# A graph-network kernel of four layers on one core: one store per batch instead of four, and a rearranged first norm and second batch norm

## Time and profile before

| what | value |
|---|---|
| median of 3 runs | 464.56 us (463.43 to 468.84) |
| time of the profiled execution | 463.99 us |
| its span, first to last instruction | 462.2 us |
| busy: PE, DVE, ACT, POOL | 442.4, 340.3, 241.0, 38.4 us |
| mean granted clock of PE | 0.984 |
| moved by DMA | 99.23 MB |

### The profile page before, as it was taken

One profiled execution on the slowest core, in us unless ns is written; L12 is line 12 of the kernel. 1 busy time (PEld: TensorE's weight loads), 2 busy tenths in 40 slices (PEclk: granted clock), 3 DMA queues, 4 the chain that ended last, 5 costly groups with the idle time before them and its releaser, 6 DMA issues.

```text
span 462.2 us, 6176 instructions
## 1 busy us (share of the span) xinstructions
PE 442.4 (96%) x2202; PEld 273.4 (59%) x2202; DVE 340.3 (74%) x725; ACT 241.0 (52%) x421; POOL 38.4 (8%) x59
## 2 busy tenths in 40 slices
PE   5999999899899999999999999999599999999996
PEld 3434434344343334878776866676267688888885
DVE  3897876899999969879779657675758785866212
ACT  3998784586798634663335436445542533511210
POOL 3330000012311200010010000100000000000000
PEclk8899999999999999999999999999889999999999
DMA  7997535123999999856099766772990740000002
GB/s 261 417 365 170 198 116 211 61 92 142 357 397 403 379 386 384 328 164 246 0 358 423 292 238 255 279 251 71 401 340 26 296 150 34 1 0 2 0 3 91
DMA packets 18906, 99.23 MB, mean 215 GB/s; under 512 B 3903, under 2 KB 4287, under 8 KB 8383
## 3 DMA queue, kind: packets, MB, share of 16 engines
q1 hardware_dynamic: 14151, 72.86, 42.2%
q0 software_dynamic: 4000, 25.18, 14.8%
q10 hardware_dynamic: 720, 0.73, 0.5%
HBM read 93.50 MB, written 5.25 MB: 214 GB/s over the span
## 4 chain that ended last, share of the span: by engine, by line
PE 82%; DMA 10%; DVE 6%; issue 1%; ACT 1%; DVEq 0%; SPq 0%; ACTq 0%
PE bank L1270 18%; PE sbank L1592 9%; DMA bring<-in_basis 9%; PE sbank L1256 8%; PE bank L1343 7%; PE sbank L1326 6%; PE bank L1605 6%; PE bank L1498 5%; PE bank L1577 5%; PE bank L1256 3%; PE bank L1310 3%; PE sbank L1236 3%; PE sbank L1310 3%; PE sbank L1381 2%; PE bank L1404 2%; PE sbank L1458 2%
## 5 line engine op out<-in xcount | busy, mean ns | idle before, releaser
L1256 PE MATMUL sbank<-bring,attw 120*32 120x512 f32 x320 | 40.3, 612 | 4.9 <-DMA bring<-in_basis 4.9
L762 DVE TENSOR_SCALAR cnt<-iota_row,edge_f 128x512 bf16<-128x512 f16 x132 | 40.8, 345 | 4.4 <-PE sbank L1326 4.4
L509 ACT ACTIVATE adjT<-distance,edge_w,edge_f 128x128 bf16<-128x128 bf16 x61 | 29.2, 480 | 2.0 <-PE sbank L1326 2.0
L1326 PE MATMUL sbank<-cnt,adjT 128*128 128x512 bf16 x132 | 30.0, 380 | 0.0
L419 ACT ACTIVATE stat<-stat,eps 128x1 f32<-128x1 f32 x32 | 9.4, 295 | 39.0 <-DVE stat L772 39.0
L1343 PE MATMUL bank<-hT,wring 128*128 128x512 f32 x64 | 28.9, 594 | 0.0
L1185 DVE SCALAR_TENSOR_TENSOR y_lo<-sbank,gate,y_hi 128x512 fp32r<-128x512 f32 x16 | 11.8, 749 | 22.6 <-ACT y_hi L690 22.6
L448 ACT ACTIVATE s<-bank,colsb 128x512 f32<-128x512 f32 x24 | 16.4, 687 | 21.8 <-PE bank L1270 21.8
L1256 PE MATMUL bank<-bring,attw 120*32 120x512 f32 x192 | 23.7, 600 | 2.6 <-DMA bring<-in_basis 2.5
L759 DVE TENSOR_SCALAR adjT<-iota_row,edge_f,edge_w 128x128 bf16<-128x128 f16 x71 | 22.1, 311 | 5.4 <-PE sbank L1326 5.4
L480 ACT ACTIVATE distance<-iota_row,edge_f 128x128 bf16<-128x128 f16 x61 | 24.3, 400 | 1.7
(11 more groups left out here) (227 smaller groups left out, 1062.8 us busy)
## 6 DMA issues: line engine op xcount, KB each, us to landing
bring<-in_basis SPq DMA_DIRECT2D x63, 1024.0 KB, 8.2
wring<-in_weights POOLq DMA_DIRECT2D x8, 1024.0 KB, 10.0
landing<-in_weights POOLq DMA_DIRECT2D x4, 1024.0 KB, 7.2
w_scratch<-stage SPq DMA_DIRECT2D x64, 64.0 KB, 8.0
hT<-in_weights POOLq DMA_DIRECT2D x4, 1024.0 KB, 10.4
qkw<-w_scratch POOLq DMA_DIRECT2D x2, 2048.0 KB, 8.1
rring<-in_rows POOLq DMA_DIRECT2D x12, 256.0 KB, 8.6
hT<-w_scratch POOLq DMA_DIRECT2D x4, 256.0 KB, 6.9
```

The costliest lines, as they stand in the source:

```text
L509: act.activation(hot_d[:, n % HOT, :], distance[:, i % 2, :], ACT.Relu, scale=minus_w[:, n:n + 1], bias=weight_f[:, n:n + 1]).then_inc(sem ...
L762: dve.tensor_scalar(hot_s[:, n % HOT, :], iota[:, :], src_f[:, n:n + 1], None, ALU.is_equal).then_inc(sem("hot_ready"), 1)
L1256: mm = pe.matmul(unit_bank(b)[32 * j:32 * j + 32, :], attw[0:KB, u // UNITS, g, :], bring[0:KB, u % BATCH, j, :], start=(g == 0), stop=(g ...
L1326: pe.matmul(bank[7][:, :], hot_d[:, n % HOT, :], hot_s[:, n % HOT, :], start=(n == 0), stop=(n == ECH - 1)).then_inc(sem("hot_used"), 1)
```

## The change

- **Stores.** SP stores a batch with one DMA instead of four. Its DRAM side has three dimensions, 4 x 32 x 512 elements, its SBUF side is 128 partitions of 512. The store of batch n // 4 - 2 is issued ahead of the load of unit n, no longer behind it. The semaphore that tells of a stored batch counts 16 instead of 64.
- **First norm.** POOL writes `eps` first. ACT takes a square root of it as soon as its DMAs are issued, into a tile that nobody reads. Square roots and the scaled ReLUs go in pairs of tiles. ACT copies turned tiles 2 and 3, DVE copies tiles 0 and 1. PE turns into banks 0 to 3, with 23 zero matmuls ahead and 0, 4, 1, 2 behind the four turns (12 and 2, 2, 2, 2 before). The first q tile comes ahead of all counts.
- **Second batch norm.** Two units instead of four stand ahead of the turns. Behind them come four units, two zero matmuls, one unit and three zero matmuls (three units before).

```diff
@@ stored()
-            return sum(b % SLOTS == slot for b in range(groups)) * COLT * 16
+            return sum(b % SLOTS == slot for b in range(groups)) * 16
@@ SP, for n in range(2 * UNITS + 2 * BATCH)
+                    if n % BATCH == BATCH - 1 and n >= 3 * BATCH - 1:
+
+                        b = n // BATCH - 2
+                        sp.wait_ge(sem("stage_ready"), b + 1)
+                        layer, g = divmod(b, BATCHES)
+                        if b == 2 * BATCHES - 1:
+                            sp.wait_ge(sem("gate_rows"), 16 * 2 * RELS)
+                        sp.dma_start(scratch[layer].rearrange("(j u) q o -> j u q o", j=COLT)[
+                            :, g * BATCH:(g + 1) * BATCH, :, :].rearrange("j g q o -> j (g q) o"),
+                            stage[:, b % SLOTS, :]).then_inc(
+                                sem(f"w_stored{b % SLOTS}"), 16)
                     if n < 2 * UNITS:
...
-                        for j in range(COLT):
-                            at = j * UNITS + g * BATCH
-                            sp.dma_start(scratch[layer, at:at + BATCH, :, :].rearrange("g q o -> (g q) o"),
-                                         stage[32 * j:32 * j + 32, b % SLOTS, :]).then_inc(
-                                             sem(f"w_stored{b % SLOTS}"), 16)
@@ POOL: memset(eps) is first, ahead of memset(zeros)
@@ ACT
+                act.activation(root_of_eps[:, :], eps[:, :], ACT.Sqrt)
+
+                def relu0(c):
                     act.wait_ge(sem("nbias0"), c + 1)
...
+                root(0, 0)
+                root(0, 1)
+                relu0(0)
+                relu0(1)
+                root(0, 2)
+                root(0, 3)
+                relu0(2)
+                relu0(3)
+                for c in (2, 3):
+                    turn("hT0", hT, c, 0, C)
@@ DVE
                 for c in range(C):
                     dve.wait_ge(sem(f"x{c}_loaded"), 16)
-                    n = step(dve.bn_stats(st(0, c, 0, 6), xr[:, c, :]))
-                    if c:
-                        nbias(0, c - 1)
-                    after(n)
-                    norm_aggr(0, c)
-                nbias(0, C - 1)
+                    norm_stats(0, xr[:, c, :], c)
+                    if c == 1:
+                        nbias(0, 0)
+                        nbias(0, 1)
+                nbias(0, 2)
+                nbias(0, 3)
+                for c in (0, 1):
+                    dve.wait_ge(sem("hT0_psum"), c + 1)
+                    dve.tensor_copy(hT[:, :, blk(P, c)],
+                                    bank[c][:, :].rearrange("p (f n) -> p f n", f=C)).then_inc(sem("hT0"), 1)
@@ PE, start
-                keep_clock(12)
+                keep_clock(23)
                 pe.wait_ge(sem("ident"), 2)
-                for c in range(C):
-                    turn(hr, c, "h0", "hT0")
-                    keep_clock(2)
+                for c, idle in enumerate((0, 4, 1, 2)):
+                    turn(hr, c, "h0", "hT0", base=0, banks=C)
+                    keep_clock(idle)
+                pe.wait_ge(sem("hT0"), C)
+                qkv_tile(0)
                 for n in range(ECH):
                     count(n)
-                    if n == first:
-                        pe.wait_ge(sem("hT0"), C)
                     t, at = divmod(n - first, every)
+                    if t == 0:
+                        continue
@@ PE, second batch norm
                 parts_stage("c2_1", x_parts, "c1_1", "c2_1_psum")
-                units(4)
+                units(2)
...
-                units(3)
+                units(4)
+                keep_clock(2, bank[4])
+                units(1)
+                keep_clock(3, bank[4])
```

More of the change, by code:

```diff
@@ L207, in build @@
         eps = sb("eps", [P, 1])
+        root_of_eps = sb("root_of_eps", [P, 1])
         distance = sb("distance", [P, 2, P], BF16)
@@ L326, in _ @@
             def _(pool):
+                pool.memset(eps[:, :], LN_EPS).then_inc(sem("eps"), 1)
                 pool.memset(zeros[:, :], 0.0).then_inc(sem("zeros"), 1)
@@ L330, in _ @@
                           allow_small_or_imprecise_dtypes=True).then_inc(sem("iota"), 1)
-                pool.memset(eps[:, :], LN_EPS).then_inc(sem("eps"), 1)
                 pool.memset(ones[:, :], 1.0).then_inc(sem("constants"), 1)
@@ L489, in _ @@
                 act.wait_ge(sem("eps"), 1)
-                for c in range(C):
-                    root(0, c)
+                act.activation(root_of_eps[:, :], eps[:, :], ACT.Sqrt)
+                def relu0(c):
                     act.wait_ge(sem("nbias0"), c + 1)
@@ L494, in _ @@
                                    bias=st(0, c, 10)).then_inc(sem("h0"), 1)
-                    if c:
-                        turn("hT0", hT, c - 1)
-                turn("hT0", hT, C - 1)
+                root(0, 0)
[8 more added lines that the diff above has]
+                    turn("hT0", hT, c, 0, C)
                 act.wait_ge(sem("edge_step"), 8)
@@ L1346, in _, with keep_clock @@
                 first, every = FIRST_TILE, TILE_EVERY
-                def keep_clock(n):
+                def keep_clock(n, to=bank[7]):
                     for _ in range(n):
-                        pe.matmul(bank[7][:, :], zeros[:, 0:P], zeros[:, :], start=True, stop=True)
+                        pe.matmul(to[:, :], zeros[:, 0:P], zeros[:, :], start=True, stop=True)
                 pe.wait_ge(sem("zeros"), 1)
-                keep_clock(12)
+                keep_clock(23)
                 pe.wait_ge(sem("ident"), 2)
-                for c in range(C):
-                    turn(hr, c, "h0", "hT0")
-                    keep_clock(2)
+                for c, idle in enumerate((0, 4, 1, 2)):
[3 more added lines that the diff above has]
+                qkv_tile(0)
                 for n in range(ECH):
                     count(n)
-                    if n == first:
-                        pe.wait_ge(sem("hT0"), C)
                     t, at = divmod(n - first, every)
+                    if t == 0:
+                        continue
                     if at == 0 and t < 2 * C:
```

## The result

The changed kernel takes **475.22 us** (median of 4 runs, 474.80 to 475.93) against 464.78 for the kernel before (4 runs, 463.43 to 468.84). The ratio of the means is 1.021, with a 95% interval of 1.015 to 1.028: slower, by about 2%. The forecast was 468.4, its range ended at 473.0. The profiled execution after took 475.93 with a span of 474.1; before it was 462.2.

What follows compares the result with a forecast made beforehand. PE holds 82% of the chain of waits, with PE, DVE and DMA nearly full in the attention. 463.99 - 3.0 (start) + 4.0 (attention) + 1.5 (unit 43) + 1.9 (second batch norm) = 468.4 us, range 456.5 to 473.0.

Steps and rivals of the forecast that it cites:

- The mechanism of the store: Stores: one DMA with four shared outermost pieces goes over four engines, 64 KB each, +1.9 us for each batch.
- Rival A: Whole kernel: the store is spread over all 16 engines and everything works as written, -6.5, 457.5 us; chance 0.25.
- If all 6.0 are slack the cost is 1.5, if none is 7.5 ... +4.0: Attention, to unit 29: dearer stores delay loads; unit 29 started 6.0 us after the loads' floor; +4.0 us taken.
- 2.5 to 5 later, +1.5, bounds 0 and +2.5: Unit 43: its load, now behind the store, lands 2.5 to 5 us later, at 249.5 to 252, wanted at 249.4.
- The start: First norm: earlier table load and ReLUs bring the first q tile and counts forward, -3.0 us, bounds -1.6 and -3.3.
- the 23 zero matmuls fill PE until about 7.7: Start: the zero matmuls ahead of the turns last until about 7.7 us, when the first ReLU ends.
- The 6 us for DVE's 16 one-hots: Start: 16 counts need 6 us of DVE, until 19.3; PE wants the last at 19.2, so DVE just keeps up.
- The second batch norm: Second batch norm: unit 59's load waits behind a store, three zero matmuls follow, clock stays low; +1.9, bounds -3.0 and +3.5.
- An earlier start of PE is therefore kept: From the start to 80 us: PE has no wait on the chain, so its gain stays as far as DVE starts earlier.
- Rival B: Attention: four engines set its whole pace, slower by over 2%, 476.9 us, or 475.5 with the full start; chance 0.10.
- part 3: The prediction's part on the second batch norm: +1.9 us forecast, +3.5 in rival B.
- Rival C: Start: it does not pay, -1.0 instead of -3.0, while the store costs as forecast; 470.4 us; chance 0.10.

## Why the prediction was wrong

**The mechanism of the store held.** The store goes over four engines, its issue takes 0.5 us, and unit 59's load decides at the second batch norm. Rival A is out in both of its halves: the store is not spread, and where it is spread (462.9 us, contiguous rows) it is not faster than four stores in the same place (463.9) by more than their intervals, where A had 457.5. The Trainium skill, page "DMA: Bandwidth & Descriptors", section "Rules for kernel authors", advises to merge small transfers. Here merging 64 KB stores into one of 256 KB gave nothing that could be measured on 16 engines, and cost 11 us on four (in the same place, ahead of the load).

**The steps that failed are two sizes and a term that was left out, 7.6 us in all.**

1. *The attention: "If all 6.0 are slack the cost is 1.5, if none is 7.5 ... +4.0".* Measured +6.1 up to unit 29, and +6.6 with the one store behind the load. The bounds held, but I took a value near the middle, with no row for it: of the 7.5 us that four stores add to four engines I counted 3.5 as slack. The five kernels with a store on four engines lost 5.3 to 6.8 us from unit 0 to unit 29, so only 0.7 to 2.2 were slack. With two engines the same sum gives 17.5 us, and the trace 16.1, so 1.4 were slack. With eight it gives 2.5, and the trace nothing. That is an estimate by my own price for a byte, and it fits: the cost is near nothing while the rings still have room, and nearly the full bytes once they have not.

2. *What a wait leaves behind was left out, although the rows had it.* I priced the lower clock at the second batch norm (0.81, 2.00 for four matmuls), and not at the two places where I was making new waits. Behind unit 29 unit and projection took 0.87 + 2.17 = 3.0 us more (that this is the clock is argued, not tried), of which 0.6 came back later; behind unit 43 the clock took 1.6, and filling that wait with zeros gave this back in the trace. Together 4.1 of the 7.6, for a term that stood in the sum at nothing.

3. *Unit 43, "2.5 to 5 later, +1.5, bounds 0 and +2.5".* The load took 5.0 us more (19.06 against 14.1), the upper end of the span, and I had taken the lower half. The shift from the wait alone came to 2.8 us, over the bound, and the clock's 1.6 came on top.

Two sizes were off by less. The start gave 2.3 and not 3.0: "the 23 zero matmuls fill PE until about 7.7" held in the run with four stores (6.42 us, to 7.8) and failed in the changed kernel's profile (8.00 us, to 9.35). From 4 to 7 us TensorE ran 9 of the zero matmuls there, and 16 in the other run. The granted clock is told as 1.00 for that stretch in both, so a lower clock that lasted longer is likely and not shown. Over the 13 profiles with the changed start unit 0 begins between 22.93 and 23.93 us, which is a gain of 2.0 to 3.0: 3.0 was the upper end. The 6 us for DVE's 16 one-hots do not follow from the rates given (16 x 0.345 and DVE's half of the other kind give about 8); in the run with four stores behind, the chain goes through them from 12.49 to 19.41, so DVE just kept up, as forecast. The second batch norm cost 1.3 and not 1.9.

"An earlier start of PE is therefore kept" failed too, though the sum hides it. With stores on four engines, unit 36 starts at 235.1 to 235.6 us with the changed start and without it.

**Rival B** is the one that came true in its result: 475.5 with the full start, against 475.22. It got 0.10. Its own marks were passed only in part: unit 29 at 171.6, not beyond 172, and its +7.5 there was really 6.1 up to unit 29 and 2.5 behind it. It also had +3.5 in part 3, where 1.3 came, and +2.5 at unit 43, where 4.5 came. The number came out right partly by luck, and the chance was still too low: B needs only that little slack is left, and a DMA share of 0.99 is a row that says so. Rival C is out as the cause: the first q tile began at 12.85, short of its 14.

## What to carry to other kernels

Before merging DMAs, count the outermost pieces of both sides of the merged one: if fewer than 16 come out, some engines get several times the bytes, and a load that is spread over all 16 lands with the slowest. Where the rings are nearly full, price those bytes in full as soon as they exceed what little room there is: 16 KB more on an engine for each store cost 0.7 us here, 32 KB on top 11, and 64 KB on top 18. Check too that a gain ahead of such a stretch gets through it. And where a change adds waits on TensorE, price the matmuls behind them at the lower clock as one bound; if a wait can't be avoided, zero matmuls in it can give the clock back (1.6 us in the trace here).

## What the runs showed that I had not expected

- The count of packets on the page tells how many engines a DMA used: 16 x 12 = 192 fewer for 16 stores on 4 engines, to the packet; and a store on fewer than 16 engines has no landing time on the page. Its semaphore has one update for each engine and one more.
- An outer count written over rows that follow on each other changes nothing (8 x 16 and 2 x 64: 463.1 and 463.2 us, 18138 packets each, destination counts [128,1]). An outer count over stretches that lie apart does.
- The DMA share of a long stretch hardly shows an uneven load: 0.97 against 0.99, while PE's waits on DMA went from 10% to 14% of the chain.
- One wait of 1.98 us left the clock up (one store behind the load), two of 1.66 and 1.45 with 1.0 us of work between them did not, nor did one of 1.88 ahead of unit 43 (four stores ahead). So the length of the wait alone does not decide it; what does was not tried.
- The start's first 23 zero matmuls took between 6.42 and 8.02 us in the 13 profiles that have them.
